# Softmax attention: VectorE adds five probability tiles, GpSimd eleven, and one wave of ones per head takes the place of six

## The chip, the cores and the metric

The kernel runs on one core of one Trainium2 chip. The metric is the device time of one execution in microseconds. The kernel before takes 5820.37 us, the median of three runs (5817.99 to 5821.75).

## The reference

The program is a chain of four layers on an input of two sequences of 2048 rows of 512 columns: a Mamba layer, a softmax attention layer, and two linear attention layers. The change lies in the second layer. Cut to what matters, it computes:

```python
q = (xn @ q_w + q_b).reshape(Bx, Tx, H, -1)      # 16 heads of 32 columns
k = (xn @ k_w + k_b).reshape(Bx, Tx, H, -1)
att = jnp.einsum('bnhl,bmhl->bnmh', q, k)
att = att + (1.0 - mask) * -1000000.0
att = jax.nn.softmax(att, axis=2)
y = jnp.einsum('bnmh,bmhl->bnhl', att, v).reshape(Bx, Tx, Dx)
```

All of it is float32. For each head and query the softmax needs the maximum over the 2048 keys, the exponentials, and their sum, the denominator.

## The kernel before

Five stages run one after the other, with a barrier of all engines between them. The change touches only `stage_attention`, which runs from about 2540 to 4370 us of the span. It treats 32 heads (two sequences by 16), one after the other, as a pipeline over heads written out by hand. Each engine has its own order of instructions, and semaphores that count upward are what couples them.

A head has 16 steps, one for each key tile of 128 keys (the code calls the tile a unit, `u` or `kt`). In step `u` the engines do this:

- **TensorE** makes the scores of unit `u + 1` of this head, transposed (128 keys by 2048 queries), in four matmuls of 512 queries (`score_mm`, line 1272), alternating with four max matmuls (`max_mm`, line 1247). These compute scores of the head after this one, 128 queries by 2048 keys, for the maximum over keys. They run three steps ahead (`LEAD`), so from step 13 on (`TURN_MAX`) they belong to the head after next. Then comes the output wave of unit `u` (`pv_mm`, line 1283): the values of 128 keys are the weights, the exponentials pass through, and four groups of 32 columns of the array take 512 queries each.
- **ScalarE** makes the exponentials of unit `u + 1` into one of four slots (`prob`, line 1342), in four instructions of 512 columns. Before it overwrites a slot it waits for the output wave and for the add of the unit that was there, four units earlier.
- **VectorE** reduces each tile of the max matmuls to its maximum (`reduce`, line 1376). There are three PSUM banks for these tiles (`BANKS`), and TensorE waits for the reduction of the tile three earlier before it writes one (`free_bank`). The same three banks also take the transposed maxima in step 13 and the transposed output in step `TURN_O`.
- **GpSimd** sums the exponentials of several units element by element, in halves of 1024 columns (line 1230). The 16 units form six groups of 2, 3, 3, 2, 3 and 3 units. Per group one wave of ones (`den_mm`, line 1293, weights of 1.0) sums the group's tile over the 128 keys on TensorE and accumulates in the bank `ps_d`. It follows the output wave two steps after the last unit of its group (`DEN_LAG`). Two sum tiles alternate. After the fourth group GpSimd copies the values of the next head (line 1215).

In step 2 of the next head (`TURN_O`) TensorE transposes the output and the denominators of the head (`turn_o`, lines 1258 and 1262), after ScalarE has copied both out of PSUM (lines 1348 and 1352), and VectorE inverts the denominators and multiplies (`read_o`, lines 1393 and 1398).

In the last head there are no more max tiles, so VectorE has no reductions left. The stage before attention, the Mamba layer, is cited for single instructions: VectorE's line 623 multiplies two SBUF tiles of 128x512, its line 630 a PSUM tile with an SBUF tile of 128x1024, and GpSimd's lines 397, 402 and 428 work on SBUF tiles beside them.

Of the kernel before, what the change touches and what calls it, by code (L numbers as in the profile page):

```python
# [9 lines left out]
ALU = mybir.AluOpType  # L10
AX = mybir.AxisListType

P = 128
NB = 2
S = 2048
D = 512
KD = D // P
CH = 512
# [913 lines left out]
QT = S // P  # L932
# [169 lines left out]
def stage_attention(nc, a, keep, parts, mask_parts, v):  # L1102

    with ExitStack() as ctx:
# [7 lines left out]
        SIZES = (2, 3, 3, 2, 3, 3)  # L1112
        GROUPS = [tuple(range(sum(SIZES[:g]), sum(SIZES[:g + 1]))) for g in range(len(SIZES))]
        NGRP = len(GROUPS)
        GROUP_END = {units[-1]: g for g, units in enumerate(GROUPS)}
        ADDS = sum(2 * (len(units) - 1) for units in GROUPS)
        used, sums = {}, {}
        for g, units in enumerate(GROUPS):
            for n, unit in enumerate(units[1:]):
                for half in range(2):  # L1120
                    used[unit, half] = 2 * sum(len(x) - 1 for x in GROUPS[:g]) + 2 * n + half + 1
                    if n == 0:
                        used[units[0], half] = used[unit, half]
                    sums[g] = used[unit, half]
# [3 lines left out]
        TURN_O = 2  # L1128
        DEN_LAG = 2
# [3 lines left out]
        pair_sum = [r.sb(f"pair_sum{i}", [P, S]) for i in range(2)]  # L1133
# [14 lines left out]
                 "o_mm o_copied sum_done den_mm den_copied den_turned den_inv den_read v_copied")  # L1148
# [64 lines left out]
        def _(pool):  # L1213
# [5 lines left out]
            for hd in range(HEADS):  # L1219
                for g, units in enumerate(GROUPS):  # L1220
                    if hd * NGRP + g >= 2:
                        pool.wait_ge(s["den_mm"], hd * NGRP + g - 1)
                    for n, unit in enumerate(units[1:]):
                        for half in range(2):
                            at = slice(half * HALF, (half + 1) * HALF)
                            pool.wait_ge(s["exp_done"], (hd * QT + unit) * QB + 2 * half + 2)
                            if n:
                                pool.wait_ge(s["sum_done"], hd * ADDS + used[units[n], half])
                            first = pair_sum[g % 2] if n else prob[units[0] % SLOTS]
                            nc.gpsimd.tensor_tensor(pair_sum[g % 2][:, at], first[:, at], prob[unit % SLOTS][:, at],  # L1230
                                                    ALU.add).then_inc(s["sum_done"], 1)
# [704 lines left out]
```

## Time and profile before

| | us |
|---|---|
| median of three runs | 5820.37 |
| the profiled execution's own time | 5820.17 |
| its span | 5818.2 |
| TensorE busy | 5255.1 (90%) |
| VectorE busy | 4103.5 (71%) |
| GpSimd busy | 3309.9 (57%) |
| ScalarE busy | 2832.8 (49%) |

The shares are means over all stages. The chain that ended last covers only the last stages, as each barrier cuts it off, and so it says nothing on attention. That stage is read from stretches of it, from the order of time within one head, and from the instructions by line. In the rows PE is TensorE, PEld its weight loads, DVE VectorE, ACT ScalarE and POOL GpSimd. The spans on GpSimd are rough.

### The profile page before, as it was taken

What the parts mean: (1) busy time and instruction counts of PE and PEld (TensorE: products, weight loads), DVE (VectorE), ACT (ScalarE), POOL (GpSimd) and SP (SyncE); (2) the same over time, 40 slices, a digit from 0 to 9 for tenths busy, and PEclk for the clock granted to TensorE, in tenths of its full rate; (3) what the DMA queues carried; (4) which work ended last, traced back from release to release, by engine and by line L of the source; (5) the groups of instructions that cost most, each with busy time, mean ns of one, the idle gap of its engine ahead of it and who ended that gap; (6) DMA issues with size and microseconds to landing.
All of it is one profiled execution on the core that took longest, in us unless ns stands there. A gap on an engine that the chain in (4) does not pass through costs nothing. (4 is left out here: it accounts for less than half of the span.)

```text
span 5818.2 us, 58795 instructions
## 1 busy us (share of the span) xinstructions
PE 5255.1 (90%) x19584; PEld 2488.2 (43%) x19584; DVE 4103.5 (71%) x5406; ACT 2832.8 (49%) x4895; POOL 3309.9 (57%) x2160
## 2 busy tenths in 40 slices
PE   6888988888898869989999999999998889989898
PEld 2333333333333324444555554555544454544545
DVE  3999999999999963367777777777744444445444
ACT  4657576675757523326666666666661121312121
POOL 4879797887979741118888888888880000000000
PEclk8999999999999999979999999999999999989999
DMA  4021221212122023321111111111103202021101
GB/s 167 22 102 36 88 94 51 77 47 102 36 87 95 29 83 136 123 70 34 23 34 23 34 34 23 34 30 27 34 1 134 91 17 69 17 103 35 60 26 51
DMA packets 116737, 346.28 MB, mean 60 GB/s; under 512 B 12273, under 2 KB 13521, under 8 KB 102033
## 3 DMA queue, kind: packets, MB, share of 16 engines
q1 hardware_dynamic: 98512, 294.46, 15.5%
q0 software_dynamic: 9216, 33.56, 1.5%
q10 hardware_dynamic: 8704, 14.50, 0.7%
q8 instruction: 155, 2.54, 0.2%
q14 instruction: 150, 1.22, 0.1%
HBM read 274.29 MB, written 67.67 MB: 59 GB/s over the span
## 5 line engine op out<-in xcount | busy, mean ns | idle before, releaser
L1376 DVE TENSOR_REDUCE attn_mx<-attn_ps_max 128x1 f32<-128x512 f32 x2048 | 1269.5, 682 | 404.7 <-PE attn_ps_max L1247 400.1
L428 POOL TENSOR_TENSOR mamba_hc<-mamba_h,mamba_bc 128x1024 f32<-128x1024 f32 x512 | 1218.0, 2379 | 359.4 <-DVE mamba_h L640 305.7
L1342 ACT ACTIVATE attn_prob<-attn_ps_s 128x512 f32<-128x512 f32 x2048 | 1061.0, 604 | 589.2 <-PE attn_ps_s L1272 586.2
L784 PE MATMUL mamba_y<-mamba_hc,ident 128*128 128x512 f32 x2048 | 995.4, 609 | 275.2 <-POOL mamba_hc L428 273.1
L1230 POOL TENSOR_TENSOR attn_pair_sum<-attn_prob 128x1024 f32<-128x1024 f32 x384 | 906.5, 2382 | 312.1 <-ACT attn_prob L1342 312.1
L534 ACT ACTIVATE mamba_da<-mamba_dt,mamba_a_neg 128x512 f32<-128x512 f32 x1024 | 691.1, 689 | 717.8 <-DVE mamba_h L640 714.2
L640 DVE TENSOR_TENSOR_SCAN mamba_h<-mamba_da,mamba_state,mamba_h 128x512 f32<-128x512 f32 x768 | 939.4, 1264 | 1.9 <-ACT mamba_da L534 1.9
L1272 PE MATMUL attn_ps_s<-attn_q_stack,attn_k_stack 100*128 100x512 f32 x2048 | 862.3, 424 | 4.2 <-ACT attn_prob L1342 4.2
L1247 PE MATMUL attn_ps_max<-attn_k_stack,attn_q_stack 98*128 98x512 f32 x2048 | 835.1, 415 | 16.3 <-DMA attn_q_stack<-qk_parts 16.2
L784 PEld LDWEIGHTS mamba_y<-mamba_hc,ident 128*128 128x128 f32 x2048 | 366.4, 191 | 856.3 <-POOL mamba_hc L428 455.5
L630 DVE TENSOR_TENSOR mamba_h<-mamba_du,mamba_bc 128x1024 f32<-128x1024 f32 x512 | 618.6, 1208 | 65.6 <-POOL mamba_state L430 57.3
L1230 POOL TENSOR_TENSOR attn_pair_sum<-attn_pair_sum,attn_prob 128x1024 f32<-128x1024 f32 x256 | 604.8, 2387 | 0.0
L1272 PEld LDWEIGHTS attn_ps_s<-attn_q_stack,attn_k_stack 100*128 100x128 f32 x2048 | 387.3, 190 | 455.6 <-ACT attn_prob L1342 232.3
L1283 PE MATMUL attn_ps_o<-attn_prob,attn_v_h 128*32 128x512 f32 x4096 | 546.3, 605 | 0.0
L1247 PEld LDWEIGHTS attn_ps_max<-attn_k_stack,attn_q_stack 98*128 98x128 f32 x2048 | 396.7, 194 | 133.0 <-DVE attn_mx L1376 40.3
L892 POOL TENSOR_TENSOR lin_norm_rstd<-lin_norm_var_eps,neg_half 128x4 f32<-128x4 f32 x16 | 16.1, 1007 | 597.7 <-DVE lin_norm_var_eps L881 597.7
L892 POOL TENSOR_TENSOR lin_out_norm_rstd<-lin_out_norm_var_eps,neg_half 128x4 f32<-128x4 f32 x16 | 16.1, 1006 | 578.0 <-DVE lin_out_norm_var_eps L881 578.0
L640 DVE TENSOR_TENSOR_SCAN mamba_h<-mamba_da,mamba_zeros,mamba_h 128x512 f32<-128x512 f32 x256 | 313.1, 1264 | 0.8 <-ACT mamba_da L534 0.8
L772 PE MATMUL mamba_work<-mamba_w,mamba_zy 128*128 128x512 f32 x512 | 251.9, 619 | 31.6 <-DVE mamba_x_in L658 31.1
L397 POOL TENSOR_TENSOR mamba_u<-mamba_u,mamba_tap 128x512 f32<-128x512 f32 x192 | 251.0, 1309 | 44.4 <-ACT mamba_tap L492 33.4
L729 PE MATMUL mamba_work<-mamba_xn_t,mamba_w 128*128 128x512 f32 x512 | 242.7, 600 | 2.4 <-ACT mamba_halo L494 1.4
L740 PE MATMUL mamba_work<-mamba_xn_t,mamba_w 128*128 128x512 f32 x512 | 242.3, 595 | 0.0
(230 smaller groups left out, 6092.7 us busy)
## 6 DMA issues: line engine op xcount, KB each, us to landing
mamba_bc<-bc_dram SPq DMA_DIRECT2D x64, 1024.0 KB, 7.2
mamba_w<-in_in_proj_w_T SPq DMA_DIRECT2D x16, 2048.0 KB, 7.9
qk_parts<-qkv_pair POOLq DMA_DIRECT2D x64, 512.0 KB
attn_k_stack<-qk_parts SPq DMA_DIRECT2D x96, 256.0 KB
attn_q_stack<-qk_parts SPq DMA_DIRECT2D x96, 256.0 KB
mamba_x_in<-in_x SPq DMA_DIRECT2D x16, 1024.0 KB, 5.3
mamba_w<-in_out_proj_w_T SPq DMA_DIRECT2D x8, 2048.0 KB, 8.4
lin_norm_x<-x_after_L SPq DMA_DIRECT2D x16, 1024.0 KB, 5.7
```

The lines of the kernel that those rows point to most:

```text
L428: nc.gpsimd.tensor_tensor(hc[:, gs % HC_SLOTS, :, :], h[:, gs % H_SLOTS, :, :], bc[:, g, G:2 * G, :], ALU.mult).then_inc(s["hc_done"], 1)
L534: nc.scalar.activation(da[n % DA_BANKS][:, :], dt[:, ct % 2, :], ACT.Exp, scale=a_neg[:, ct, g * G + j:g * G + j + 1]).then_inc(s["exp_don ...
L630: nc.vector.tensor_tensor(h[:, gs % H_SLOTS, :, :], du[:, :].unsqueeze(1).to_broadcast([P, G, CH]), bc[:, g, 0:G, :], ALU.mult).then_inc(s ...
L640: nc.vector.tensor_tensor_scan(h[:, gs % H_SLOTS, j, :], da[(gs * G + j) % DA_BANKS][:, :], h[:, gs % H_SLOTS, j, :], first, ALU.mult, ALU ...
L772: mm = nc.tensor.matmul(at("out", it, t)[:, :], zy[:, k, t * P:(t + 1) * P], w_view("out", it)[:, k, :], start=(k == 0), stop=(k == CT - 1))
L784: mm = nc.tensor.matmul(y[ct % 2][:, :], ident[:, :], hc[:, gs % HC_SLOTS, j, :], start=(g == 0 and j == 0), stop=(g == NG - 1 and j == G ...
L1230: nc.gpsimd.tensor_tensor(pair_sum[g % 2][:, at], first[:, at], prob[unit % SLOTS][:, at], ALU.add).then_inc(s["sum_done"], 1)
L1247: nc.tensor.matmul(free_bank(seq)[:, :], q_st[slot][0:ROWS_MAX, qt * P:(qt + 1) * P], k_st[slot][0:ROWS_MAX, kc * CH:(kc + 1) * CH], start ...
L1272: nc.tensor.matmul(ps_s[n % BANKS][:, :], k_st[slot][0:ROWS, kt * P:(kt + 1) * P], q_st[slot][0:ROWS, c * CH:(c + 1) * CH], start=True, st ...
L1283: mm = nc.tensor.matmul(ps_o[c * DH1:(c + 1) * DH1, :], v_h[hd % 3][:, kt, :], prob[kt % SLOTS][:, c * CH:(c + 1) * CH], start=(kt == 0), ...
L1342: nc.scalar.activation(prob[kt % SLOTS][:, c * CH:(c + 1) * CH], ps_s[n % BANKS][:, :], ACT.Exp).then_inc(s["exp_done"], 1)
L1376: nc.vector.tensor_reduce(mx[hd % 3][:, qt, kc:kc + 1], ps_max[seq % BANKS][:, :], AX.X, ALU.max).then_inc(s["bank_read"], 1)
```

## The change

The sum of the exponentials of one head is divided between two engines. VectorE adds up units 2, 3, 7, 10 and 13 in a tile of its own, `dve_sum`, in halves of 1024 columns. Its adds stand in steps 3, 7, 10 and 13, the first half behind the second reduction of the step and the second half behind the fourth. GpSimd adds up the other eleven units in one sum tile per head, of which there are two. In step 2 of the next head VectorE adds its sum to GpSimd's (`join_sums`), at the same two places between reductions. One wave of ones follows in step 3 (`DEN_AT`), and the transposes and `read_o` move from step 2 to step 4 (`TURN_O`). GpSimd copies the next head's values after its first unit. ScalarE waits for the adds of either engine, according to the unit. The semaphore `sum_done` becomes `pool_added` and `dve_added`.

```diff
@@ -1109,28 +1109,27 @@
         NMAX = QT * QB
         PER = NMAX // QT
         LEAD = 3
-        SIZES = (2, 3, 3, 2, 3, 3)
-        GROUPS = [tuple(range(sum(SIZES[:g]), sum(SIZES[:g + 1]))) for g in range(len(SIZES))]
-        NGRP = len(GROUPS)
-        GROUP_END = {units[-1]: g for g, units in enumerate(GROUPS)}
-        ADDS = sum(2 * (len(units) - 1) for units in GROUPS)
-        used, sums = {}, {}
-        for g, units in enumerate(GROUPS):
-            for n, unit in enumerate(units[1:]):
-                for half in range(2):
-                    used[unit, half] = 2 * sum(len(x) - 1 for x in GROUPS[:g]) + 2 * n + half + 1
-                    if n == 0:
-                        used[units[0], half] = used[unit, half]
-                    sums[g] = used[unit, half]
+        DVE_UNITS = (2, 3, 7, 10, 13)
+        POOL_UNITS = tuple(u for u in range(QT) if u not in DVE_UNITS)
+        DVE_ADDS, POOL_ADDS = 2 * len(DVE_UNITS), 2 * (len(POOL_UNITS) - 1)
+        WAVES = 1
+
+        def used(unit, half):
+
+            units = DVE_UNITS if unit in DVE_UNITS else POOL_UNITS
+            return 2 * max(units.index(unit) - 1, 0) + half + 1
+
         SLOTS = 4
         HEADS = NB * H1
         TURN_MAX = QT - LEAD
-        TURN_O = 2
-        DEN_LAG = 2
+        TURN_O = 4
+        DEN_AT = 3
+        JOIN_AT = 2
...
-        pair_sum = [r.sb(f"pair_sum{i}", [P, S]) for i in range(2)]
+        pool_sum = [r.sb(f"pool_sum{i}", [P, S]) for i in range(2)]
+        dve_sum = r.sb("dve_sum", [P, S])
...
             for hd in range(HEADS):
-                for g, units in enumerate(GROUPS):
-                    if hd * NGRP + g >= 2:
-                        pool.wait_ge(s["den_mm"], hd * NGRP + g - 1)
-                    for n, unit in enumerate(units[1:]):
-                        for half in range(2):
-                            at = slice(half * HALF, (half + 1) * HALF)
-                            pool.wait_ge(s["exp_done"], (hd * QT + unit) * QB + 2 * half + 2)
-                            if n:
-                                pool.wait_ge(s["sum_done"], hd * ADDS + used[units[n], half])
-                            first = pair_sum[g % 2] if n else prob[units[0] % SLOTS]
-                            nc.gpsimd.tensor_tensor(pair_sum[g % 2][:, at], first[:, at], prob[unit % SLOTS][:, at],
-                                                    ALU.add).then_inc(s["sum_done"], 1)
-                    if g == NGRP // 2 and hd + 1 < HEADS:
+                if hd >= 2:
+                    pool.wait_ge(s["den_mm"], (hd - 1) * WAVES)
+                for n, unit in enumerate(POOL_UNITS[1:]):
+                    for half in range(2):
+                        at = slice(half * HALF, (half + 1) * HALF)
+                        pool.wait_ge(s["exp_done"], (hd * QT + unit) * QB + 2 * half + 2)
+                        if n:
+                            pool.wait_ge(s["pool_added"], hd * POOL_ADDS + used(POOL_UNITS[n], half))
+                        first = pool_sum[hd % 2] if n else prob[POOL_UNITS[0] % SLOTS]
+                        nc.gpsimd.tensor_tensor(pool_sum[hd % 2][:, at], first[:, at], prob[unit % SLOTS][:, at],
+                                                ALU.add).then_inc(s["pool_added"], 1)
+                    if n == 0 and hd + 1 < HEADS:
                         take_v(hd + 1)
...
-            def den_mm(hd, g):
-
-                if g == 0 and hd:
+            def den_mm(hd):
+
+                if hd:
                     pe.wait_ge(s["den_read"], hd)
-                pe.wait_ge(s["sum_done"], hd * ADDS + sums[g])
+                pe.wait_ge(s["dve_added"], (hd + 1) * DVE_ADDS)
                 for c in range(QB):
                     mm = nc.tensor.matmul(ps_d[c * DH1:(c + 1) * DH1, :], ones[:, :],
-                                          pair_sum[g % 2][:, c * CH:(c + 1) * CH], start=(g == 0), stop=(g == NGRP - 1))
+                                          pool_sum[hd % 2][:, c * CH:(c + 1) * CH], start=True, stop=True)
...
                     pv_mm(hd, u)
-                    if u >= DEN_LAG and u - DEN_LAG in GROUP_END:
-                        den_mm(hd, GROUP_END[u - DEN_LAG])
-                    elif u < DEN_LAG and hd and u - DEN_LAG + QT in GROUP_END:
-                        den_mm(hd - 1, GROUP_END[u - DEN_LAG + QT])
+                    if u == DEN_AT and hd:
+                        den_mm(hd - 1)
...
                     before, unit = divmod(hd * QT + kt - SLOTS, QT)
-                    act.wait_ge(s["sum_done"], before * ADDS + used[unit, c // 2])
+                    if unit in DVE_UNITS:
+                        act.wait_ge(s["dve_added"], before * DVE_ADDS + used(unit, c // 2))
+                    else:
+                        act.wait_ge(s["pool_added"], before * POOL_ADDS + used(unit, c // 2))
...
+            def add_own(hd, unit, half):
+
+                at = slice(half * HALF, (half + 1) * HALF)
+                n = DVE_UNITS.index(unit) - 1
+                dve.wait_ge(s["exp_done"], (hd * QT + unit) * QB + 2 * half + 2)
+                if n:
+                    dve.wait_ge(s["dve_added"], hd * DVE_ADDS + used(DVE_UNITS[n], half))
+                    first = dve_sum
+                else:
+                    if hd:
+                        dve.wait_ge(s["dve_added"], hd * DVE_ADDS)
+                    first = prob[DVE_UNITS[0] % SLOTS]
+                nc.vector.tensor_tensor(dve_sum[:, at], first[:, at], prob[unit % SLOTS][:, at],
+                                        ALU.add).then_inc(s["dve_added"], 1)
+
+            def join_sums(hd, half):
+
+                at = slice(half * HALF, (half + 1) * HALF)
+                dve.wait_ge(s["pool_added"], hd * POOL_ADDS + used(POOL_UNITS[-1], half))
+                dve.wait_ge(s["dve_added"], hd * DVE_ADDS + used(DVE_UNITS[-1], half))
+                nc.vector.tensor_tensor(pool_sum[hd % 2][:, at], pool_sum[hd % 2][:, at], dve_sum[:, at],
+                                        ALU.add).then_inc(s["dve_added"], 1)
...
             for hd in range(HEADS):
                 for u in range(QT):
-                    for j, tile in enumerate(max_tiles(hd, u)):
-                        reduce(item_at(hd, "max", u, j), *tile)
+                    tiles = max_tiles(hd, u)
+                    for j in range(PER):
+                        if tiles:
+                            reduce(item_at(hd, "max", u, j), *tiles[j])
+                        if j % 2 and u in DVE_UNITS[1:]:
+                            add_own(hd, u, j // 2)
+                        if j % 2 and u == JOIN_AT and hd:
+                            join_sums(hd - 1, j // 2)
                     if u == TURN_O and hd:
                         read_o(item_at(hd, "turn_o", u), hd - 1)
                     if u == TURN_MAX and hd + 1 < HEADS:
                         second_part(item_at(hd, "turn_max", u), hd + 1)
+            for half in range(2):
+                join_sums(HEADS - 1, half)
             read_o(first_item[HEADS], HEADS - 1)
```

## Rows read from the trace of the kernel before

**Rows 1.** Busy time 2650 to 3200: PE, PEld, DVE, ACT, POOL; granted clock, DMA share, GB/s.

```profile
2650.00:3200.00 550.00, 549.96 (x3100) 275.83 (x3103) 407.13 (x675) 340.82 (x665) 470.55 (x209) 1.00 0.12 28
```

**Rows 2.** Groups by line and form, 2650 to 4300: busy us, mean ns, idle before.

```profile
L1376 DVE TENSOR_REDUCE attn_mx<-attn_ps_max 128x1 f32<-128x512 f32 x1902 | 1180.2, 682 | 384.6 <-PE attn_ps_max L1247 380.4
...
L1342 ACT ACTIVATE attn_prob<-attn_ps_s 128x512 f32<-128x512 f32 x1903 | 985.8, 604 | 545.6 <-PE attn_ps_s L1272 542.6
...
L1230 POOL TENSOR_TENSOR attn_pair_sum<-attn_prob 128x1024 f32<-128x1024 f32 x358 | 845.3, 2383 | 237.6 <-ACT attn_prob L1342 237.6
...
L1247 PEld LDWEIGHTS attn_ps_max<-attn_k_stack,attn_q_stack 98*128 98x128 f32 x1903 | 361.0, 190 | 91.1 <-DVE attn_mx L1376 17.8 <-DVE v L1398 12.9
...
L1293 PE MATMUL attn_ps_d<-attn_pair_sum,attn_ones 128*32 128x512 f32 x1424 | 185.3, 592 | 0.0
```

**Rows 3.** Order of time, TensorE, three steps: start, length, instruction.

```profile
3389.63 0.50 PE L1272 MATMUL attn_ps_s<-attn_q_stack,attn_k_stack 100*128 100x512 f32 x1
...
3389.97 0.40 PE L1247 MATMUL attn_ps_max<-attn_k_stack,attn_q_stack 98*128 98x512 f32 x1
...
3391.37 0.39 PE L1247 MATMUL attn_ps_max<-attn_k_stack,attn_q_stack 98*128 98x512 f32 x1
...
3392.69 0.50 PE L1272 MATMUL attn_ps_s<-attn_q_stack,attn_k_stack 100*128 100x512 f32 x1
...
3396.60 0.50 PE L1272 MATMUL attn_ps_s<-attn_q_stack,attn_k_stack 100*128 100x512 f32 x1
```

**Rows 4.** Order of time, the other engines in the first of these steps.

```profile
3390.17 2.07 ACT L1342 ACTIVATE attn_prob<-attn_ps_s 128x512 f32<-128x512 f32 x4 [1.00 <-PE attn_ps_s L1272]
...
3390.40 2.48 DVE L1376 TENSOR_REDUCE attn_mx<-attn_ps_max 128x1 f32<-128x512 f32 x4 [0.58 <-PE attn_ps_max L1247]
...
3391.40 4.72 POOL L1230 TENSOR_TENSOR attn_pair_sum<-attn_prob 128x1024 f32<-128x1024 f32 x2 [1.80 <-ACT attn_prob L1342]
```

**Rows 5.** Order of time, TensorE: output waves on either side of the eight transposes.

```profile
3435.93 1.06 PE L1283 MATMUL attn_ps_o<-attn_prob,attn_v_h 128*32 128x512 f32 x8
...
3440.24 1.06 PE L1283 MATMUL attn_ps_o<-attn_prob,attn_v_h 128*32 128x512 f32 x8
```

**Rows 6.** The tile of the output copies: minimum, median and maximum ns, first and last start.

```profile
L1348 ACT ACTIVATE attn_o_raw<-attn_ps_o x32: 597/598/598, 2649.4 to 4360.5; 128x512 f32<-128x512 f32 x32
```

**Rows 7.** Single lines over the whole span: minimum, median and maximum ns.

```profile
L623 DVE TENSOR_TENSOR mamba_du<-mamba_dt,mamba_u x64: 664/671/1845, 91.7 to 2089.6; 128x512 f32<-128x512 f32 x64
...
L397 POOL TENSOR_TENSOR mamba_u<-mamba_u,mamba_tap x192: 1259/1272/1779, 45.5 to 1853.7; 128x512 f32<-128x512 f32 x192
...
L428 POOL TENSOR_TENSOR mamba_hc<-mamba_h,mamba_bc x512: 2329/2352/2729, 99.8 to 2121.4; 128x1024 f32<-128x1024 f32 x171
...
L630 DVE TENSOR_TENSOR mamba_h<-mamba_du,mamba_bc x512: 1189/1210/1226, 93.6 to 2115.3; 128x1024 f32<-128x1024 f32 x171
...
L1804 DVE TENSOR_TENSOR lin_q<-lin_q,lin_q_red x16: 2291/2292/2294, 4587.4 to 5680.5; 128x2048 f32<-128x2048 f32 x16
...
L1091 DVE TENSOR_TENSOR qkv_pair<-qkv_full,qkv_pair x64: 678/691/694, 2188.0 to 2517.5; 128x512 fp32r<-128x512 f32 x64
```

**Rows 8.** Order of time, VectorE and GpSimd in the stage before attention.

```profile
244.14 1.84 DVE L623 TENSOR_TENSOR mamba_du<-mamba_dt,mamba_u 128x512 f32<-128x512 f32 x1
...
244.14 2.96 POOL L397 TENSOR_TENSOR mamba_u<-mamba_u,mamba_tap 128x512 f32<-128x512 f32 x2
...
661.47 0.67 DVE L623 TENSOR_TENSOR mamba_du<-mamba_dt,mamba_u 128x512 f32<-128x512 f32 x1
...
661.63 2.72 POOL L428 TENSOR_TENSOR mamba_hc<-mamba_h,mamba_bc 128x1024 f32<-128x1024 f32 x1 [1.00 <-DVE mamba_h L640]
```

**Rows 9.** Order of time, GpSimd in head 31: its first and last adds.

```profile
4307.24 4.71 POOL L1230 TENSOR_TENSOR attn_pair_sum<-attn_prob 128x1024 f32<-128x1024 f32 x2 [0.66 <-ACT attn_prob L1342]
...
4360.53 4.63 POOL L1230 TENSOR_TENSOR attn_pair_sum<-attn_pair_sum,attn_prob 128x1024 f32<-128x1024 f32 x2
```

**Rows 10.** Busy time in ten microseconds of a later stage (PEclk is the granted clock).

```profile
5414.00:5424.00 10.00, 2.67 (x14) 2.51 (x14) 5.99 (x14) 1.28 (x1) 1.01 (x1) 0.75 0.01 2
```

More of the change, by code:

```diff
@@ L1147, in stage_attention @@
         names = ("ones_set rows_set max_in bank_filled bank_read m_done m_first m_second s_mm exp_done "
-                 "o_mm o_copied sum_done den_mm den_copied den_turned den_inv den_read v_copied")
+                 "o_mm o_copied pool_added dve_added den_mm den_copied den_turned den_inv den_read v_copied")
         s = {n: r.sem(n) for n in names.split()}
@@ L1323, in _ @@
                         turn_max(item_at(hd, "turn_max", u), hd + 1)
-            den_mm(HEADS - 1, NGRP - 1)
+            den_mm(HEADS - 1)
             turn_o(first_item[HEADS], HEADS - 1)
@@ L1350, in copy_den @@
             def copy_den(hd):
-                act.wait_ge(s["den_mm"], (hd + 1) * NGRP)
+                act.wait_ge(s["den_mm"], (hd + 1) * WAVES)
                 nc.scalar.activation(d_raw[:, :], ps_d[:, :], ACT.Copy).then_inc(s["den_copied"], 1)
```

## The prediction

> **What bounds the kernel now.** I read the busy table over three stretches of 550 us of the attention stage first; they are alike, and one stands in the rows. TensorE is busy for practically the whole stretch and keeps its full clock, VectorE has a quarter idle and GpSimd a seventh [rows 1]. So a microsecond less of TensorE work is a microsecond gained, as long as nothing else becomes late. The per-line groups say what is in it [rows 2]. The order of time then gives the pace. A step of one key tile (unit) starts with its first score matmul; without a wave of ones the next starts 3.06 us later (3389.63 to 3392.69), with one 3.91 us (to 3396.60) [rows 3]. So a wave costs 0.85 us. The four transposes of the output and four of the denominator stretch the distance of two output waves from 3.06 to 4.31 us, so they cost 1.25 [rows 5]. One head takes (4360.5 - 2649.4) / 31 = 55.2 us from the trace of the output copies [rows 6]; 16 x 3.06 + 6 x 0.85 + 1.25 gives 55.3.
>
> Within a step, from its start at 0 [rows 3, 4]: the first of four max matmuls goes out at 0.34, the fourth at 1.74; VectorE's four reductions start at 0.77 and follow each other every 0.60 us (2.48 less one of 0.68, by three); GpSimd, when it is idle, starts at 1.77 on the unit whose exponentials are just coming; and the next step starts 1.32 after the last max matmul (3391.37 to 3392.69). VectorE then stands idle for 0.58 us. GpSimd's two halves follow each other every 4.72 - 2.38 = 2.34 us [rows 2, 4].
>
> **The change, part by part.**
>
> *Waves of ones.* Five of six go in each head: 5 x 0.85 = 4.25 us. On the path as long as TensorE is full. That would leave 55.2 - 4.25 = 50.95 us a head.
>
> *GpSimd.* Still 20 adds of 128x1024 a head (ten further units by two halves, as the six groups had), 20 x 2.34 = 46.8, and the copy of v. By itself that fits in 50.95. It waits for no wave of ones within a head any more: worth nothing, as its idle time ends on exponentials [rows 2].
>
> *VectorE.* It gets ten adds of 128x1024 a head: two in each of steps 3, 7, 10, 13, and the two joins in step 2. No row shows one here. Two operands in SBUF take 0.691 us for 512 columns and 2.292 for 2048 [rows 7], so 1024 take 0.691 + 1.601/3 = 1.22, and at the 0.08 by which neighbours overlap the next instruction starts 1.14 after. Ten are 11.4 us, and VectorE's idle share is (1 - 407/550) x 55.2 = 14 us [rows 1]: by shares it fits. But the idle time can't be saved up. There are three banks for max tiles, so TensorE is never more than three tiles ahead, and the fourth max matmul of the next step waits for that step's first reduction, which is queued behind both adds. With the first add at 0.77 + 1.20 = 1.97, two reductions to 4.31, the second add to 5.45, the next reduction done at 6.13 and 1.32 + 0.03 behind it, two steps take 7.48 instead of 6.12: 1.36 lost at each of steps 7, 10 and 13. In the pair 2 and 3, four adds and six reductions follow without a pause: the last add ends at 10.13, the reduction at 10.81, and step 5 starts at 10.84 + 1.32 + 1.25 = 13.41 instead of 3 x 3.06 + 0.85 + 1.25 = 11.28: 2.13 lost. So even with adds that nothing disturbs, a head takes 50.95 + 3 x 1.36 + 2.13 = 57.2 us. That is the lower bound of this part.
>
> *VectorE against GpSimd.* The stage before attention holds one VectorE instruction with two SBUF inputs beside GpSimd adds (line 623). Its median is 0.671 us, its longest 1.845 [rows 7]. One long case starts at 244.14, together with a GpSimd add of 512 columns: it ends at 245.98, which is one GpSimd add (1.27, 0.04 less for the overlap) and its own 0.63 on; and GpSimd's next add, which had been queued, takes the rest of 2.96 for the two. The longest add of that line is 1.779 against a median of 1.272: 0.51 lost [rows 7, 8]. The other order is there too: the VectorE instruction of 661.47 came first, keeps its 0.67, and GpSimd's multiplication of 661.63 takes 2.72 instead of 2.35 [rows 7, 8]. The control is line 630, whose first operand is in PSUM: 512 times between 1.189 and 1.226 beside the same GpSimd work [rows 7]. So the two engines exclude each other for a whole instruction where VectorE reads two SBUF operands; and between two queued GpSimd instructions VectorE gets its turn. All ten new adds are of this kind. (The Trainium skill, page SBUF — State Buffer, in the section with the diagram of the ports, says that such an instruction and a GpSimd one that reads SBUF hold a shared pair of ports exclusively, and the other "fully blocks". The trace agrees, but for the size on GpSimd's side: 0.51 lost to an instruction of 0.67. By the page GpSimd would need 46.8 + 10 x 1.22 + 0.6 = 59.6 us a head, an estimate; by the rows 57.8, below.)
>
> An add of 1024 columns keeps GpSimd out for 0.51 + 0.53 (512 more columns) = 1.04. GpSimd so needs 46.8 + 0.6 + 10.4 = 57.8 us a head, above 55.2 already. The waits of VectorE cost more, as they stand in front of its reductions:
>
> Step 7, 10 or 13: GpSimd has emptied its queue (the last unit's halves end 4.68 after 1.77, so 0.33 into the second step after) and starts the first half of the next unit at 1.77, 0.20 before VectorE asks at 1.97. VectorE gets in at 4.11; two reductions from 5.25 to 6.45; GpSimd's second half, let in at 5.15, holds until 7.49; the second add runs until 8.63, the next reduction is done at 9.31, and the step after next starts at 9.34 + 1.32 = 10.66. Loss 10.66 - 6.12 = 4.5.
>
> Steps 2 and 3: GpSimd has nothing to do in step 2 (units 2 and 3 are VectorE's), so both joins run at once, until 5.45. GpSimd starts unit 4 at 3.06 + 1.77 = 4.83, is let in at 5.35 and holds until 7.69; the third add asks at 6.65, runs 7.69 to 8.83; GpSimd's other half holds from 8.73 to 11.07; the fourth runs until 12.21; the reduction is done at 12.89, and step 5 starts at 12.92 + 1.32 + 1.25 = 15.5. Loss 4.2.
>
> *Other moves, at nothing.* The one wave of ones now waits for the joins; they are done at 5.5 while TensorE comes to it at about 7 in step 3. Its copy is made by ScalarE in step 3, in its idle time (604 x 4 = 2.4 us of work in a step of 3.06 or more [rows 2]). Transposes move from step 2 to 4. ScalarE waits for the adds of the unit four earlier: in the schedule above each is done more than a step before. If GpSimd fell behind by two steps, this cover would be gone and the head would be at GpSimd's 57.8 or more, still under the sum.
>
> *Sum.* A head takes 50.95 + 3 x 4.5 + 4.2 = 68.65 us, 13.45 more than now. Heads 1 to 29: 29 x 13.45 = 390. Head 0 has no joins: 4 x 4.5 - 4.25 = 13.75. In head 30 step 13 has no reductions left: 13.45 - 4.5 = 8.95. Head 31 has none at all and is paced by GpSimd's adds, which run until 4365.16 [rows 9], 57.9 us from its first at 4307.24; then 57.2 and a join: 0.5. Together 413. The profiled execution's span 5818.2 becomes 6231, and its time 5820.2 (2.0 outside the span, and the median of the runs within 0.2) becomes 6233.
>
> **Rivals.**
> (a) GpSimd and VectorE meet in a luckier order. The case rests on 0.20 us. With VectorE first: first add 1.97 to 3.11, GpSimd 3.01 to 5.35, second add until 6.49, loss 8.52 - 6.12 = 2.4. A head is 68.65 - 3 x 2.1 = 62.35, +7.15; times 30.5 heads +218: 6038. Against it: GpSimd's start at 1.77 is the same in every step where it waits for an exponential [rows 4].
> (b) The adds don't exclude each other here: 57.2 a head, +2.0, 30.5 heads: +60, 5880. Against it: rows 8.
> (c) The other side, faster: VectorE's adds fit in its idle quarter, TensorE stays full, and the waves are saved: 31 x 4.25 = 132, 5688. For it: the shares [rows 1], and that TensorE bounds. It decides once the losses per head fall below 4.25; even with undisturbed adds they are 6.2, since three banks don't carry the lead that would be needed.
> (d) TensorE's clock falls as well. It would stand still for some 2 us twice around each add step, and be busy for 6.1 of 10.7 us. In ten microseconds after 5414, of which it was busy for 2.7, the granted clock was 0.75, so half of them at 1.2 GHz instead of 2.4 [rows 10]. That costs about 2.5 us each time. Four times a head it would be 10 us, +310: 6540; every second time 6390. Against it: twice as much work as in that row, with matmuls between the stops.
>
> **Chances and range.** A difference under 0.2% (12 us) can't be told from none. Forecast (6150 to 6310) 0.62; (a) or a mix with it 0.16; (b) 0.06; (c) 0.05, of which 0.01 ends at no change; (d) 0.11. The range reaches over (a), and to the lower end of (d): 6000 to 6340. Faster 0.04, same 0.01, slower 0.95.
>
> **What would show it.** In the profile after: distance of two output copies 68 to 69 us; TensorE busy under 85% of the attention stage; ones matmuls 256 instead of 1536; VectorE adds with a shortest of 1.2 us, a mean of 2.3 (3.3 and 2.2 in steps 7, 10, 13; 1.2 for joins) and about 740 us in all; GpSimd adds with some 8 in 20 at 3.4 us instead of 2.38; weight loads of the max matmuls waiting for VectorE, 3 us or more an add step, where they now wait 17.8 us in 30 heads [rows 2]. Joins well over 1.3 us, or ScalarE waiting for GpSimd's sums, would show GpSimd behind, against my schedule. Adds all near 1.2 would show (b); a granted clock under 0.97, (d).

## The result: 12.8% slower, and the profile after

| | before | after |
|---|---|---|
| median, us | 5819.18 (4 runs) | 6565.18 (4 runs, 6535.72 to 6582.76) |
| profiled execution's span, us | 5818.2 | 6552.0 |
| TensorE's mean granted clock | 0.977 | 0.907 |

The ratio is 1.1279, with a 95% interval of 1.1254 to 1.1304. The forecast was 6233, with a range of 6000 to 6340. The direction and most of the mechanism were right; the time is close to that of rival (d), 6540, which had a chance of 0.11.

The same 550 us of the attention stage as in [rows 1], in the kernel after. The columns are busy us (and instructions) of TensorE, its weight loads, VectorE, ScalarE and GpSimd, then the granted clock:

```profile
2650.00:3200.00 550.00, 453.94 (x1906) 214.31 (x1902) 439.87 (x542) 253.53 (x468) 386.53 (x146) 0.82 0.09 21
```

TensorE, which was full, now stands still for 96 of 550 us, and its clock is 0.82 on average instead of 1.00. VectorE went from 407 to 440 us busy, although much of that is waiting, as the next view shows. The groups by line, from 2650 to 5000, answer to [rows 2]; the lines have moved by a few numbers:

```profile
L1228 POOL TENSOR_TENSOR attn_pool_sum<-attn_pool_sum,attn_prob 128x1024 f32<-128x1024 f32 x535 | 1502.3, 2836 | 537.3 <-ACT attn_prob L1341 536.6
L1375 DVE TENSOR_REDUCE attn_mx<-attn_ps_max 128x1 f32<-128x512 f32 x1904 | 1211.2, 682 | 379.6 <-PE attn_ps_max L1245 373.4 <-DVE attn_m_parts L1382 0.5
...
L1400 DVE TENSOR_TENSOR attn_dve_sum<-attn_dve_sum,attn_prob 128x1024 f32<-128x1024 f32 x177 | 475.1, 2684 | 0.0
L1245 PEld LDWEIGHTS attn_ps_max<-attn_k_stack,attn_q_stack 98*128 98x128 f32 x1906 | 427.3, 224 | 650.8 <-DVE attn_mx L1375 530.0 <-DVEq L1386 61.9 <-DVE v L1420 2.2
...
L1400 DVE TENSOR_TENSOR attn_dve_sum<-attn_prob 128x1024 f32<-128x1024 f32 x60 | 131.6, 2193 | 0.0
...
L1408 DVE TENSOR_TENSOR attn_pool_sum<-attn_pool_sum,attn_dve_sum 128x1024 f32<-128x1024 f32 x60 | 72.9, 1215 | 0.0
...
L1291 PE MATMUL attn_ps_d<-attn_pool_sum,attn_ones 128*32 128x512 f32 x240 | 31.2, 592 | 0.0
```

The joins (line 1408) take 1.215 us each, what an add of 1024 columns needs by itself. The adds of line 1400 are the same work and take 2.19 and 2.68 us on average. TensorE's weight loads wait 530 us for the reductions (17.8 us in [rows 2]). The ones matmuls are down to 240 in 30 heads. VectorE's adds and joins come to 743 us over the whole span (513.0 + 143.5 + 86.6), with about 740 forecast. The distance of the output copies, which was 55.2 us in [rows 6], is (5084.9 - 2670.2) / 31 = 77.9:

```profile
L1347 ACT ACTIVATE attn_o_raw<-attn_ps_o x32: 597/598/601, 2670.2 to 5084.9; 128x512 f32<-128x512 f32 x32
```

In what follows, an add site is a place where VectorE makes its adds: step 7, step 10, step 13, or steps 2 and 3 taken together. From the start of step 7 to the start of step 9 of one head, VectorE in order of time (start, length, instruction):

```profile
3414.57 1.29 DVE L1375 TENSOR_REDUCE attn_mx<-attn_ps_max 128x1 f32<-128x512 f32 x2 [0.59 <-PE attn_ps_max L1245]
3415.77 3.19 DVE L1400 TENSOR_TENSOR attn_dve_sum<-attn_dve_sum,attn_prob 128x1024 f32<-128x1024 f32 x1
3418.89 1.28 DVE L1375 TENSOR_REDUCE attn_mx<-attn_ps_max 128x1 f32<-128x512 f32 x2
3420.09 2.18 DVE L1400 TENSOR_TENSOR attn_dve_sum<-attn_dve_sum,attn_prob 128x1024 f32<-128x1024 f32 x1
3422.19 2.47 DVE L1375 TENSOR_REDUCE attn_mx<-attn_ps_max 128x1 f32<-128x512 f32 x4
3426.78 0.69 DVE L1375 TENSOR_REDUCE attn_mx<-attn_ps_max 128x1 f32<-128x512 f32 x1 [2.12 <-PE attn_ps_max L1245]
```

VectorE's first add takes 3.19 us, as it asks 0.27 us after GpSimd has started its own, and the second takes 2.18. GpSimd runs four adds around them and needs 11.30 us instead of 4 x 2.34 = 9.4:

```profile
3415.50 11.30 POOL L1228 TENSOR_TENSOR attn_pool_sum<-attn_pool_sum,attn_prob 128x1024 f32<-128x1024 f32 x4 [1.85 <-ACT attn_prob L1341]
```

The step after next starts 12.21 us after the first (3414.57 to 3426.78). I had worked out 10.66 and, undisturbed, 6.12. What the other 1.55 us are, the clock shows: first three stretches of these steps, then one behind step 10, and those behind steps 13 and 3 of the same turn of the loop (columns as above, the clock is third from the right):

```profile
3411.00:3418.00 7.00, 6.82 (x35) 3.39 (x34) 5.92 (x7) 4.73 (x10) 5.15 (x4) 1.00 0.00 0
3418.00:3424.00 6.00, 2.41 (x9) 1.09 (x13) 6.00 (x8) 1.67 (x3) 6.00 (x2) 0.89 0.00 0
3424.00:3431.00 7.00, 7.00 (x27) 3.30 (x20) 3.43 (x6) 2.53 (x5) 2.80 (x2) 0.61 0.00 1
...
3436.00:3443.00 7.00, 5.51 (x15) 2.33 (x16) 5.18 (x7) 1.33 (x3) 7.00 (x3) 0.52 0.00 0
...
3376.00:3383.00 7.00, 7.00 (x27) 3.25 (x27) 4.65 (x8) 2.88 (x5) 4.11 (x2) 0.59 0.76 174
...
3404.00:3411.00 7.00, 7.00 (x33) 4.32 (x26) 3.63 (x7) 2.29 (x4) 4.32 (x2) 0.64 0.00 0
```

It is 1.00 up to 3418 in the steps just shown (3411 to 3418). TensorE is then busy for 2.41 of 6 us, and the clock falls to 0.89 on average and to 0.61 in the next seven microseconds: most of that stretch is at 1.2 GHz. It is just the stretch in which TensorE has work that others wait for, and the reductions there follow each other every 0.85 us instead of 0.60, at the pace of the matmuls. The other rows are the same behind the three other add sites, 0.52 to 0.64.

### The profile page after: what moved, and what is told of

It reads as the page before. It is cut to its first block and busy times, and to the rows that moved or that the text cites. A ratio compares the mean times of both kernels' runs of the same rounds, so it can differ in the third digit from the quotient of the medians.

```text
span 6552.0 us, 57033 instructions
## 1 busy us (share of the span) xinstructions
PE 5573.6 (85%) x18304; PEld 2591.7 (40%) x18304; DVE 4829.0 (74%) x5726; ACT 2891.6 (44%) x4895; POOL 3571.5 (55%) x2160
## 5 line engine op out<-in xcount | busy, mean ns | idle before, releaser
L1228 POOL TENSOR_TENSOR attn_pool_sum<-attn_pool_sum,attn_prob 128x1024 f32<-128x1024 f32 x576 | 1615.8, 2833 | 560.9 <-ACT attn_prob L1341 560.3
L1341 ACT ACTIVATE attn_prob<-attn_ps_s 128x512 f32<-128x512 f32 x2048 | 1120.5, 600 | 1210.4 <-PE attn_ps_s L1270 1161.9
L1245 PE MATMUL attn_ps_max<-attn_k_stack,attn_q_stack 98*128 98x512 f32 x2048 | 997.8, 494 | 443.7 <-DVE attn_mx L1375 377.1
L1270 PE MATMUL attn_ps_s<-attn_q_stack,attn_k_stack 100*128 100x512 f32 x2048 | 973.5, 478 | 6.8 <-ACT attn_prob L1341 5.9
L1245 PEld LDWEIGHTS attn_ps_max<-attn_k_stack,attn_q_stack 98*128 98x128 f32 x2048 | 464.6, 227 | 713.5 <-DVE attn_mx L1375 573.5
L1270 PEld LDWEIGHTS attn_ps_s<-attn_q_stack,attn_k_stack 100*128 100x128 f32 x2048 | 452.3, 221 | 552.9 <-ACT attn_prob L1341 272.3
L1281 PE MATMUL attn_ps_o<-attn_prob,attn_v_h 128*32 128x512 f32 x4096 | 670.5, 733 | 0.0
L1400 DVE TENSOR_TENSOR attn_dve_sum<-attn_dve_sum,attn_prob 128x1024 f32<-128x1024 f32 x192 | 513.0, 2673 | 8.5 <-ACT attn_prob L1341 8.2
L1228 POOL TENSOR_TENSOR attn_pool_sum<-attn_prob 128x1024 f32<-128x1024 f32 x64 | 151.1, 2382 | 218.8 <-ACT attn_prob L1341 218.8
L729 PE MATMUL mamba_work<-mamba_xn_t,mamba_w 128*128 128x512 f32 x512 | 242.6, 600 | 2.5 <-ACT mamba_halo L494 1.4
```

Source lines behind the costliest of these rows:

```text
L1228: nc.gpsimd.tensor_tensor(pool_sum[hd % 2][:, at], first[:, at], prob[unit % SLOTS][:, at], ALU.add).then_inc(s["pool_added"], 1)
L1245: nc.tensor.matmul(free_bank(seq)[:, :], q_st[slot][0:ROWS_MAX, qt * P:(qt + 1) * P], k_st[slot][0:ROWS_MAX, kc * CH:(kc + 1) * CH], start ...
L1270: nc.tensor.matmul(ps_s[n % BANKS][:, :], k_st[slot][0:ROWS, kt * P:(kt + 1) * P], q_st[slot][0:ROWS, c * CH:(c + 1) * CH], start=True, st ...
L1281: mm = nc.tensor.matmul(ps_o[c * DH1:(c + 1) * DH1, :], v_h[hd % 3][:, kt, :], prob[kt % SLOTS][:, c * CH:(c + 1) * CH], start=(kt == 0), ...
L1341: nc.scalar.activation(prob[kt % SLOTS][:, c * CH:(c + 1) * CH], ps_s[n % BANKS][:, :], ACT.Exp).then_inc(s["exp_done"], 1)
L1400: nc.vector.tensor_tensor(dve_sum[:, at], first[:, at], prob[unit % SLOTS][:, at], ALU.add).then_inc(s["dve_added"], 1)
```

## The experiments

Eight kernels ran. "Head" is the mean distance of the output copies over 31 heads in each profile, and the clock is TensorE's mean granted clock in a stretch of 550 us of the stage.

| kernel | median us | ratio to before (95%) | head us | clock of the stage |
|---|---|---|---|---|
| before | 5817 to 5819 | 1 | 55.2 | 1.00 |
| the change | 6565.2 | 1.128 | 77.9 | 0.82 |
| filler matmuls in the stops | 6339.9 | 1.0896 (1.0880 to 1.0913) | 71.4 | 0.97 |
| GpSimd's adds 8 columns wide | 5910.2 | 1.0156 (1.0139 to 1.0173) | 58.3 | 0.99 |
| VectorE's adds 8 columns wide | 6082.9 | 1.0453 (1.0420 to 1.0487) | 64.0 | 0.92 |
| an operand in PSUM | 6076.9 | 1.0445 (1.0429 to 1.0460) | 62.3 | 0.96 |
| adds earlier and later in the step | 6156.7 | 1.0579 (1.0561 to 1.0597) | 65.4 | 0.93 |
| no VectorE adds | 5695.6 | 0.9790 (0.9776 to 0.9805) | 51.3 | 1.00 |
| five groups, all on GpSimd | 5802.3 | 0.9976 (0.9966 to 0.9986) | 54.6 | 1.00 |
| four groups, all on GpSimd | 5859.5 | 1.0074 (1.0059 to 1.0089) | 56.6 | 1.00 |

### Filler matmuls: is it the clock?

```diff
+            FILL = (0, 7, 1, 8)
+            def fill(hd, u, n):
...
+                slot = (hd + 1) % 3
+                for _ in range(n):
+                    nc.tensor.matmul(ps_d[:, :], q_st[slot][0:ROWS_MAX, 0:P], k_st[slot][0:ROWS_MAX, 0:CH], start=True, stop=True)
...
+                        if tiles and u - 1 in DVE_UNITS[1:]:
+                            fill(hd, u, FILL[c])
                         if tiles:
                             max_mm(item_at(hd, "max", u, c), *tiles[c])
```

> The changed kernel with filler matmuls (98x128 by 512, into the idle denominator bank) in TensorE's stops behind each pair of adds: seven before the second, one before the third and eight before the fourth max matmul of steps 8, 11 and 14, eight before the fourth in step 4. Theory: of the 77.9 us of a head, 9.3 are the clock, which falls to 1.2 GHz after the stops. With the stops filled the granted clock of the stage goes from 0.82 to 0.95 or more, a head takes 69 to 71 us, the kernel 6280 to 6350. Rival: the surplus over my schedule is a wait that I priced too low, and the low clock hides in it; then the clock rises but the time stays at 6565 or grows by the fillers.

The kernel does more work and is 225 us faster than the change (6339.9). The clock of the stage is back at 0.97:

```profile
3200.00:3750.00 550.00, 519.88 (x2493) 289.96 (x2486) 478.86 (x589) 267.15 (x506) 424.95 (x159) 0.97 0.11 24
```

The same adds at the same places, in steps 7 to 9 of one head:

```profile
3415.71 1.29 DVE L1391 TENSOR_REDUCE attn_mx<-attn_ps_max 128x1 f32<-128x512 f32 x2 [0.59 <-PE attn_ps_max L1245]
3416.92 3.20 DVE L1416 TENSOR_TENSOR attn_dve_sum<-attn_dve_sum,attn_prob 128x1024 f32<-128x1024 f32 x1
...
3421.23 2.20 DVE L1416 TENSOR_TENSOR attn_dve_sum<-attn_dve_sum,attn_prob 128x1024 f32<-128x1024 f32 x1
...
3426.29 2.48 DVE L1391 TENSOR_REDUCE attn_mx<-attn_ps_max 128x1 f32<-128x512 f32 x4 [0.46 <-PE attn_ps_max L1245]
```

They take as long as in the change, 3.20 and 2.20 us. But two steps take 10.58 us (3415.71 to 3426.29), where I had worked out 10.66 for the full clock and the change needs 12.21. So the exclusion was sized right, and what these steps lose beyond it is the clock. A head comes to 71.4, a little over the 69 to 71 expected. Where the surplus over the schedule lies can be read by cutting one head at the first reductions of steps 2, 6, 10, 13 and 0 of the next head. First the change, then the fillers:

```profile
3390.33 1.29 DVE L1375 TENSOR_REDUCE attn_mx<-attn_ps_max 128x1 f32<-128x512 f32 x2 [0.58 <-PE attn_ps_max L1245]
...
3411.49 2.48 DVE L1375 TENSOR_REDUCE attn_mx<-attn_ps_max 128x1 f32<-128x512 f32 x4 [0.84 <-PE attn_ps_max L1245]
...
3431.09 1.29 DVE L1375 TENSOR_REDUCE attn_mx<-attn_ps_max 128x1 f32<-128x512 f32 x2 [1.06 <-PE attn_ps_max L1245]
...
3446.36 1.29 DVE L1375 TENSOR_REDUCE attn_mx<-attn_ps_max 128x1 f32<-128x512 f32 x2 [0.33 <-PE attn_ps_max L1245]
...
3462.71 2.48 DVE L1375 TENSOR_REDUCE attn_mx<-attn_ps_max 128x1 f32<-128x512 f32 x4 [0.84 <-PE attn_ps_max L1245]
```

```profile
3394.11 1.29 DVE L1391 TENSOR_REDUCE attn_mx<-attn_ps_max 128x1 f32<-128x512 f32 x2 [0.59 <-PE attn_ps_max L1245]
...
3412.64 2.48 DVE L1391 TENSOR_REDUCE attn_mx<-attn_ps_max 128x1 f32<-128x512 f32 x4 [0.46 <-PE attn_ps_max L1245]
...
3429.37 1.29 DVE L1391 TENSOR_REDUCE attn_mx<-attn_ps_max 128x1 f32<-128x512 f32 x2 [0.60 <-PE attn_ps_max L1245]
...
3443.01 1.29 DVE L1391 TENSOR_REDUCE attn_mx<-attn_ps_max 128x1 f32<-128x512 f32 x2 [0.32 <-PE attn_ps_max L1245]
...
3459.97 2.48 DVE L1391 TENSOR_REDUCE attn_mx<-attn_ps_max 128x1 f32<-128x512 f32 x4 [0.58 <-PE attn_ps_max L1245]
```

| us | by the schedule | the change | with fillers |
|---|---|---|---|
| step 2 to step 6 | 15.5 + 3.06 = 18.6 | 21.16 | 18.53 |
| step 7 to step 10 | 10.66 + 3.06 = 13.72 | 16.52 | 13.66 |
| step 10 to step 13 | 10.66 + 3.06 = 13.72 | 15.27 | 13.64 |
| step 13 to step 0 of the next head | 10.66 + 3.06 = 13.72 | 16.35 | 16.96 |

The change loses 2.6, 2.8, 1.55 and 2.6 us over the schedule at its four add sites. With the fillers the first three losses are gone, 6.95 us together, and those stretches fit the schedule within 0.1 us. The fourth stays, and so does its low clock. Behind step 13 the fillers don't keep the clock up, while it is 1.00 in the other three stretches:

```profile
3440.00:3450.00 10.00, 7.78 (x38) 4.29 (x37) 9.64 (x11) 5.28 (x11) 7.74 (x4) 0.95 0.00 0
3450.00:3460.00 10.00, 10.00 (x46) 6.24 (x44) 6.18 (x11) 3.94 (x8) 5.32 (x2) 0.88 0.62 139
```

Step 13 also has a wait that the others lack: there the bank with the transposed maxima is read behind both adds, and the max matmuls of step 14 wait for it. In the change this wait has a row of its own (total, times, longest us):

```profile
PEld attn_ps_max L1245 <- DVEq L1386: 61.9, 30, 2.1
```

That is 2 us a head for a wait which my working left out. Part of it lies within the 4.5 us of the site, and the fillers of step 14 stand in its way, so this run doesn't divide the 2.6 us of step 13 between the wait and the clock.

### GpSimd's adds 8 columns wide: what do VectorE's adds cost undisturbed?

```diff
+            nc.gpsimd.memset(pool_sum[0][:, :], 1.0)
+            nc.gpsimd.memset(pool_sum[1][:, :], 1.0)
...
-                        at = slice(half * HALF, (half + 1) * HALF)
+                        at = slice(half * HALF, half * HALF + 8)
```

> GpSimd's adds cover 8 columns instead of 1024 (most of its sum is left out); VectorE's ten adds of 1024 stay. Theory: the exclusion of the two engines costs 11.5 us a head (and through the longer stops the clock's 9.3), the three banks 6.2. So VectorE's adds take 1.2 us all, a head 57 us, the kernel 5870 to 5900, clock near 1.00. Rival: it is the two adds in VectorE's own order that cost, with or without GpSimd: over 6200.

5910.2, a little over the upper end. The clock stays up, and TensorE is busy for 508 of 550 us:

```profile
3200.00:3750.00 550.00, 507.56 (x2557) 243.44 (x2556) 487.80 (x732) 330.36 (x630) 72.36 (x199) 0.99 0.12 27
```

```profile
3382.38 1.29 DVE L1377 TENSOR_REDUCE attn_mx<-attn_ps_max 128x1 f32<-128x512 f32 x2 [0.58 <-PE attn_ps_max L1247]
3383.59 1.21 DVE L1402 TENSOR_TENSOR attn_dve_sum<-attn_dve_sum,attn_prob 128x1024 f32<-128x1024 f32 x1
...
3385.92 1.21 DVE L1402 TENSOR_TENSOR attn_dve_sum<-attn_dve_sum,attn_prob 128x1024 f32<-128x1024 f32 x1
...
3393.06 1.29 DVE L1377 TENSOR_REDUCE attn_mx<-attn_ps_max 128x1 f32<-128x512 f32 x2 [0.59 <-PE attn_ps_max L1247]
```

All adds take 1.21 us. From step 7 to step 9 it takes 10.68 - 3.07 = 7.6 us (3382.38 to 3393.06 are three steps, one of them plain), against 7.48 worked out. From step 13 to step 15 it takes 8.18 (3403.74 to 3411.92), 0.6 more, and there the weight loads wait for the bank with the transposed maxima, 31.4 us in 29 heads. So the two adds inside VectorE's order cost some 7 us a head by themselves (58.3 - 51.3), more than the 4.25 that the waves give. Even if GpSimd never stood in the way, the change would have lost.

### VectorE's adds 8 columns wide: a miss that shows the wait bare

```diff
-                at = slice(half * HALF, (half + 1) * HALF)
+                at = slice(half * HALF, half * HALF + 8)
                 n = DVE_UNITS.index(unit) - 1
```

(The same in `join_sums`.)

> VectorE's ten adds cover 8 columns instead of 1024 (most of its sum and of the joins is left out); GpSimd's twenty stay, and so do all waits, the one wave and the later transposes. Theory: the waits and moves cost nothing, so TensorE is full again at 50.95 us a head, GpSimd busy for 47.4 of it: 5680 to 5710. Rival: the wait for GpSimd's last unit at the joins, or the late wave, costs by itself: 5820 or more.

6082.9: the expectation was wrong, and so was the rival's reason. Three adds of one head:

```profile
3373.06 0.16 DVE L1408 TENSOR_TENSOR attn_pool_sum<-attn_pool_sum,attn_dve_sum 128x8 f32<-128x8 f32 x1
...
3392.04 2.12 DVE L1400 TENSOR_TENSOR attn_dve_sum<-attn_dve_sum,attn_prob 128x8 f32<-128x8 f32 x1
...
3395.29 1.20 DVE L1400 TENSOR_TENSOR attn_dve_sum<-attn_dve_sum,attn_prob 128x8 f32<-128x8 f32 x1
```

A join, made while GpSimd is idle, takes 0.16 us. The adds of 8 columns beside GpSimd take 2.12 and 1.20 us. They are nearly nothing but wait: 2.12 is about the 2.14 us from VectorE's asking at 1.97 to the end of GpSimd's half at 4.11, both from the schedule. That VectorE moves 128 times less data doesn't free it from the wait. I had taken it that a small instruction would slip through; it doesn't. Each stands in front of the reductions until GpSimd's instruction of 2.34 us is done, and with these stops the clock is 0.92.

### No VectorE adds: what is the single wave worth?

```diff
-                nc.vector.tensor_tensor(dve_sum[:, at], first[:, at], prob[unit % SLOTS][:, at],
-                                        ALU.add).then_inc(s["dve_added"], 1)
+                dve.sem_inc(s["dve_added"], 1)
```

(The same in `join_sums`.)

> VectorE's ten adds and joins are replaced by bare semaphore increments at the same places and behind the same waits (its sum is left out whole). The run with 8 columns showed that an add's wait for GpSimd doesn't depend on its size (2.13 and 1.20 us for 0.15 us of work), so it did not tell what the single wave is worth. Theory: with no instruction that has to wait for GpSimd, TensorE is full, a head takes 50.95 us, the kernel 5680 to 5710, which is the saving of five waves of 0.85 us. Rival: the waits at the joins, the late wave or the later transposes cost something by themselves: 5740 or more.

5695.6, as expected. TensorE is full at the full clock, and a head takes 51.3 us against 50.95:

```profile
3200.00:3750.00 550.00, 546.19 (x2908) 282.19 (x2907) 437.08 (x725) 365.67 (x714) 504.36 (x224) 1.00 0.15 33
```

So the waits, the later transposes and the single wave cost next to nothing, and five waves are worth 55.2 - 51.3 = 3.9 us a head. It is the price of rival (c), and it needs VectorE's work to vanish.

### An operand in PSUM: is it what the add reads?

```diff
+                if n and hd:
+                    two = lambda t: t[:, at].rearrange("p (g c) -> p g c", c=CH)
+                    nc.vector.tensor_tensor(two(dve_sum), ps_d[:, :].unsqueeze(1).to_broadcast([P, 2, CH]),
+                                            two(prob[unit % SLOTS]), ALU.add).then_inc(s["dve_added"], 1)
+                    return
```

(And `read_o` sets `ps_d` to 1.0 after it has read it.)

> In steps 7, 10 and 13 VectorE's adds read the denominator bank in PSUM (set to 1.0 after it was read, 0.6 us a head) in place of their own running sum in SBUF, so the running sum is left out; size, place and waits stay, and steps 2 and 3 are as in the changed kernel. Theory: with one operand in PSUM nothing excludes GpSimd, so these adds take 1.2 us instead of 3.2 and 2.2, the three sites lose 1.4 us each instead of 4.5, and only steps 3 and 4 still let the clock fall: a head of 59.5 to 62, the kernel 5950 to 6040. Rival: the adds are slowed by GpSimd's traffic in SBUF whatever they read, or by waiting for semaphores: the durations stay over 2 us and the time over 6400.

The mechanism came out as expected, the time a little higher (6076.9, head 62.3 against 59.5 to 62); no run divides this surplus. By line and form, 2650 to 4600:

```profile
L1228 POOL TENSOR_TENSOR attn_pool_sum<-attn_pool_sum,attn_prob 128x1024 f32<-128x1024 f32 x558 | 1390.0, 2524 | 319.2 <-ACT attn_prob L1341 318.9
...
L1402 DVE TENSOR_TENSOR attn_dve_sum<-attn_ps_d,attn_prob 128x1024 f32<-128x1024 f32 x186 | 225.3, 1212 | 13.3 <-ACT attn_prob L1341 13.2
...
L1405 DVE TENSOR_TENSOR attn_dve_sum<-attn_prob 128x1024 f32<-128x1024 f32 x62 | 136.0, 2195 | 0.1
```

Same size, same place, same waits, the same GpSimd beside it: with one operand in PSUM an add takes 1.212 us, with two in SBUF (only step 3 is left) 2.195. And GpSimd's adds are down from 2.836 to 2.524 us. So what matters is not the size or the place of the add, nor the semaphores it waits for. This run also takes one of VectorE's reads out of SBUF, so alone it doesn't rule out traffic. The run with 8 columns does: there the traffic is nearly gone and the wait is still 2.12 us. Together they leave the two SBUF operands on VectorE beside GpSimd as the cause.

### Adds earlier and later in the step: does the order matter?

```diff
-                        if j % 2 and u in DVE_UNITS[1:]:
+                        if j in (0, 3) and u in DVE_UNITS[1:]:
```

> The changed kernel, with VectorE's own adds one reduction earlier and one later: the first half behind the first reduction of the step (asks at 1.37 us, before GpSimd starts at 1.77), the second half behind the fourth. Joins as they were. Theory: VectorE comes first, the first add runs from 1.37 to 2.51, GpSimd's half from 2.41 to 4.75, the second add asks at 4.31, runs until 5.89, the reduction is done at 6.57 and the step after next starts at 7.9 instead of 10.7: a loss of 1.8 us at each of three sites in place of 4.5. Steps 2 and 3 stay. A head of 60.5 us at the full clock, 62.5 if one stop in step 4 still lets it fall: 6000 to 6060. Rival: GpSimd is busy so much that the order changes little: over 6400.

6156.7, 408 us better than the change, but over the 6000 to 6060 expected. Two sites of one head:

```profile
3421.66 0.69 DVE L1375 TENSOR_REDUCE attn_mx<-attn_ps_max 128x1 f32<-128x512 f32 x1 [0.59 <-PE attn_ps_max L1245]
3422.27 1.21 DVE L1400 TENSOR_TENSOR attn_dve_sum<-attn_dve_sum,attn_prob 128x1024 f32<-128x1024 f32 x1
...
3425.20 1.61 DVE L1400 TENSOR_TENSOR attn_dve_sum<-attn_dve_sum,attn_prob 128x1024 f32<-128x1024 f32 x1
...
3431.32 0.69 DVE L1375 TENSOR_REDUCE attn_mx<-attn_ps_max 128x1 f32<-128x512 f32 x1 [2.11 <-PE attn_ps_max L1245]
...
3435.69 0.69 DVE L1375 TENSOR_REDUCE attn_mx<-attn_ps_max 128x1 f32<-128x512 f32 x1 [1.12 <-PE attn_ps_max L1245]
...
3443.69 2.48 DVE L1375 TENSOR_REDUCE attn_mx<-attn_ps_max 128x1 f32<-128x512 f32 x4 [0.46 <-PE attn_ps_max L1245]
```

The adds take 1.21 and 1.61 us instead of 3.2 and 2.2: VectorE does come first. At the second site two steps take 8.00 us (3435.69 to 3443.69), where I had 7.92. At the first they take 9.66 (3421.66 to 3431.32), and the reductions after it (from 3431.32 on) come every 0.85 us, the mark of the low clock. So the miss is again the clock: 0.93 in the stage. It falls at one stop and not at the next of the same length, although TensorE is busy for 2.6 us of each (3425 to 3429 and 3439 to 3443). The runs don't tell why.

### Five and four groups, all on GpSimd

```diff
-        SIZES = (2, 3, 3, 2, 3, 3)
+        SIZES = (3, 3, 3, 3, 4)
```

(Sum tiles alternate over all groups, as five is odd. For four groups the sizes are 4, 4, 4, 4.)

> The kernel before with five groups of 3, 3, 3, 3 and 4 units in place of six: GpSimd makes 22 adds a head instead of 20, VectorE none, TensorE one wave fewer. Theory: GpSimd needs 22 x 2.34 + 0.6 = 52.1 us of a head of 55.2 - 0.85 = 54.35, so it keeps up and the wave is saved in 31 heads: 26 us, 5790 to 5800. Rival: at 96% GpSimd can't keep the order of the slots, ScalarE waits for it: 5818 or more.

> The kernel before with four groups of four units: GpSimd makes 24 adds a head, TensorE four waves. Theory: GpSimd's 24 x 2.34 + 0.6 = 56.8 us a head become the bound instead of 53.5 for TensorE: +1.6 us a head against 55.2, 5860 to 5900, and GpSimd busy for nearly the whole stage. Rival: GpSimd's adds can be shorter when they are not let wait, and TensorE still bounds: 5770.

GpSimd's busy time is the last of the five. Five groups, then four:

```profile
3200.00:3750.00 550.00, 548.43 (x3055) 275.83 (x3052) 411.44 (x681) 343.73 (x670) 522.53 (x231) 1.00 0.14 30
```

```profile
3200.00:3750.00 550.00, 528.68 (x2881) 261.70 (x2881) 398.29 (x659) 333.18 (x650) 550.00 (x244) 1.00 0.13 30
```

With five groups GpSimd is busy for 522 of 550 us and TensorE stays full: 5802.3, 15 us faster than before (0.9976, interval 0.9966 to 0.9986). The expectation was 5790 to 5800: a head takes 54.6 instead of 54.35, which is 9 of the 11 us that are missing from one wave's 26. With four groups GpSimd is busy for all of 550 us, a head takes 56.6 us where 24 x 2.34 + 0.6 = 56.8 was worked out, and the kernel is 0.7% slower than before: 5859.5, with 5860 to 5900 expected. Five groups is the only version run that keeps the whole computation, drops a wave and beats both kernels.

## Why the prediction was wrong in its size

**Bound, saving, moves: right.** TensorE at 50.95 us a head without five waves; measured 51.3 with VectorE's adds gone.

**Three banks don't carry the adds: right.** Undisturbed adds were to cost 6.2 us a head; measured 58.3 - 51.3 = 7.0. Of the 0.8 us between them 0.6 lie at step 13, where the schedule left out the wait for the transposed maxima.

**The exclusion: right, to a tenth of a microsecond.** Adds of 3.3 and 2.2 us were forecast for steps 7, 10 and 13 and measured at 3.19 and 2.18, joins of 1.2 at 1.22. Two steps at the full clock: 10.66 worked out, 10.58 measured with the fillers; steps 2 to 6: 18.6 and 18.53. GpSimd lost (11.30 - 9.4) / 2 = 0.95 us per VectorE add, against 1.04. That GpSimd would come first by 0.20 us held throughout: the mean of 2.68 over 177 adds is the mean of 3.18 and 2.18. Rival (a) was the better order, not the actual one.

**The step that failed is the clock**, rival (d). It was put aside with "twice as much work as in that row, with matmuls between the stops". The matmuls between the stops didn't hold it: four stretches at 1.2 GHz come with each head, as (d) had it, one behind each add site. The sum counts heads 1 to 29 in full. Such a head takes (4963.9 - 2670.2) / 29 = 79.1 us against (4260.2 - 2649.4) / 29 = 55.5 before, by the starts of the output copies. That is 23.55 more, where the sum had 13.45 and (d) would have added 10: 10.1 are missing, and over 29 heads they are 293 of the missing 332 us. With the fillers such a head takes (4760.0 - 2664.2) / 29 = 72.3, so 6.8 of the 10.1 come back. In the head laid out above, 6.95 of 9.6 us lie at the add sites of steps 2 and 3, 7 and 10, and there the fillers bring the time back to the schedule: this part is shown to be the clock. The 2.6 us at step 13 hold the low clock and the wait for the transposed maxima, and how they divide stays open. Rival (d)'s 2.5 us at each site compare with 2.6, 2.8, 1.55 and 2.6, the last of them not the clock alone, so that its sum of 10 fits so closely is in part luck. The forecast took stops worked out for one clock, and gave the matmuls behind them the same clock. It should have asked of each stop whether the clock outlives it: the price had been read from a row, and it was the chance that was too low.

**Small terms.** Head 0 took 20.8 us more, not 13.75 (first output copy at 2670.2 instead of 2649.4); it has the same four add sites. Heads 30 and 31 took 20.7 more (121.0 from 4963.9 to 5084.9, against 100.3), and after the last output copy come 9.4 more (6552.0 - 5084.9 against 5818.2 - 4360.5): GpSimd, slowed by the adds, ends the last head late, and the joins follow. For these 30.1 us I had 9.45. The profiled execution is also 11.4 us under the median of its runs, and with this the 332 us are complete (293 + 7 + 21 + 11).

## What to carry to other kernels

A share of idle time on an engine is no room for work when short buffers tie its order to the bottleneck: work out the two steps around the insertion, not the sum over the loop. Before VectorE is given an elementwise instruction with both operands in SBUF beside a busy GpSimd, add the two engines' times as if they were one, and count with a wait of up to GpSimd's instruction length. Here a smaller VectorE instruction didn't lower that wait, and one operand in PSUM removed it. When a change makes a full TensorE wait in the middle of its loop, price the clock with the stop: here it was four low stretches in each head.

## What the runs showed of the hardware

An 8-column add on VectorE, 0.16 us when GpSimd is idle, takes 2.12 us beside a GpSimd add. The same 1024-column add takes 2.2 to 3.2 us with two SBUF operands and 1.21 with one in PSUM. Behind each of the four add sites of the change TensorE's granted clock fell to 1.2 GHz for most of seven microseconds (0.52 to 0.64 on average). With the adds earlier and later in the step it fell behind one stop and not behind the next of the same length. With up to sixteen more matmuls in the stops behind an add site, whose results nobody reads, it stayed at 1.00 behind three of the four in the head shown, and the kernel became 225 us faster.
